# Output projection of an attention layer with its operands exchanged and y split in two float32r parts

## The chip, the cores and the metric

The program runs on one core of a Trainium2 chip. A core has four compute engines that run their own instruction streams and meet only at semaphores: TensorE (PE in the profile; its weight loads are the lane PEld), VectorE (DVE), ScalarE (ACT) and GpSimd (POOL). SyncE (SP) issues the DMAs. The metric is the device time of one execution in microseconds (us).

## The reference

Input x has 32 batches of 256 tokens of width 128. Five blocks follow each other, each on a layer norm of x and added to x: a tanh feed-forward, a linear attention, the tanh feed-forward again, a spectral (circulant) layer, a 16-head causal softmax attention, and the spectral layer again. The change touches the end of the softmax attention:

```
att = einsum('bhcq,bhCq->bhcC', q, k) / d_query        # 16 heads, 64 wide
p   = softmax(where(causal, att, -inf))
y   = einsum('bhcC,bhCv->bhcv', p, v)
z   = einsum('dvh,bhcv->bcd', W, y) * (sqrt(d_embed/d_value) / num_heads)
x   = x + z
```

So z of one batch is a product of a 256 x 1024 matrix y (tokens by heads and value channels) with a 1024 x 128 matrix W.

## The kernel before

The first four blocks run in some 260 us, in groups of 512 tokens. The softmax attention then takes the 32 batches one after another, in about 30 us each, and this is where most of the time lies. All operands stay in SBUF.

**Turns.** A batch has 8 pairs of heads, and each engine's program has 8 turns p = 0..7 for it (ACT and DVE are written in steps of two turns). In turn p of pair n = 8b + p, TensorE issues in this order: the q/k product of pair n + 2 (`qk_product`, 6 matmuls); one extra piece (values of this or the next batch in turns 0, 1, 6, 7; transposes of the next x in turn 2; the output projection of batch b - 1 in turns 3, 4, 5); the six transposes of the probabilities of pair n - 1 (`probs_transpose`); and in odd turns the scores of pairs n + 1 and n + 2 (`scores`), then the products of probabilities and values of pairs n - 2 and n - 1 (`products`). Every order is written out by hand; nothing is scheduled by a tool.

**The other engines.** DVE masks scores and finds their maxima (`mask_scores`, L527), takes the reciprocal of the sums (`inv_sum`, L535), copies two thirds of the transposed probabilities out of PSUM (`probs_T`, L542), makes the low part of q and k (`qk_low`, L513), and does the layer norms and additions to x. ACT does the exponentials (L809), the copies of q and k (L781, L787, L793, L794), one third of the transposed probabilities (L818) and the copy of y (`y_out`, L835). POOL multiplies the probabilities by the reciprocals (`scale_probs`, L333 and L335, 128x256 and 128x512) and does the small powers of the layer norms (L318, L345).

**Split operands.** TensorE's q/k and value products use float32r operands in two parts, `hi` (rounded) and `lo` (the rest), and three matmuls: hi by hi, hi by lo, lo by hi. The output projection before is in plain float32: `project_out` (L1120 to L1127) makes 16 matmuls for a batch. For each half of the tokens and each pair, 128 tokens of `yT` are the stationary operand and the 128 columns of `wz` move. The trace records each of these as two matmuls, so 32 records for a batch: 12 in turn 3, 12 in turn 4, 8 in turn 5. The result stands in PSUM with tokens on the partitions, as x does, and DVE adds it to x (`add_z`, L555).

**What orders the work around it.** `project_out` in turn 3 waits for `x_lo` of the next batch (DVE L507), as both use bank BANK_X; `x_lo` waits for ACT's `z_xT` copy (L849) and that for PE's transposes in turn 2. `y_out` of ACT writes a ring of two batches of y straight from PSUM. In turn 5 the spectral product of batch b - 2 (L1137, L1140) follows the projection, and DVE adds both results to x.

Of the kernel before, what the change touches and what calls it, by code (L numbers as in the profile page):

```python
# [17 lines left out]
G = 16  # L18
# [97 lines left out]
def build(nc, x, Wq, bq, Wd, bd, Wu, bu, Wo, bo, W1, W2, W3, ffn_bias, Q, K, V, W, w_re, w_im, fft_bias, dft, out):  # L116
    ctx = ExitStack()
    with ctx:
# [20 lines left out]
        space = sb("space", [P, 2 * BT * H * DV + 2 * PAIRS * T])  # L139
# [11 lines left out]
        wz = sb("wz", [P, PAIRS, D])  # L151
# [14 lines left out]
        xl_hi = sb("xl_hi", [P, 2, GW], F32R); xl_lo = sb("xl_lo", [P, 2, GW], F32R)  # L166
        eq = sb("eq", [P, GW]); rq = sb("rq", [P, GW]); ek = sb("ek", [P, GT, P])
        phq = sb("phq", [P, 2, GW]); phk = sb("phk", [P, GT, P])
# [3 lines left out]
        y0 = sb("y0", [P, GT, P]); yT0 = sb("yT0", [P, GW])  # L172
# [5 lines left out]
        pr = sb("pr", [P, 3, 2, 3, P])  # L178
        pT = sb("pT", [P, 2, 2, 3, P])

        vv = space[:, 0:2 * BT * H * DV].rearrange("p (r t n) -> p r t n", r=2, t=BT)
        y_ring = space[:, 2 * BT * H * DV:]
        yT = y_ring.rearrange("p (r a t) -> p r a t", r=2, a=PAIRS)
# [21 lines left out]
        pv_done = sem("pv_done"); y_ready = sem("y_ready")  # L205
# [49 lines left out]
        W_STEPS = ((0, 6), (6, 12), (12, 16))  # L255
# [28 lines left out]
        def _(pool):  # L284
# [5 lines left out]
            nc.gpsimd.memset(minus_1[:], -1.0)  # L290
            nc.gpsimd.memset(ones_bf[:], 1.0)
# [57 lines left out]

            def batch(b, jb, first=False, last=False):  # L350
# [7 lines left out]
            batches(pool, batch)  # L358
            z_inv_std(B - 1)
# [3 lines left out]
        def _(dve):  # L363
# [229 lines left out]

            def first_norm():
# [9 lines left out]
                          (1, 1): lambda: qk_weights_low(0), (1, G - LEAD - 1): lambda: qk_weights_low(1), (2, -LEAD): v_weights_low,  # L604
# [8 lines left out]
            def batch(b, jb, first=False, last=False):  # L613
                for p in range(0, PAIRS, 2):
# [22 lines left out]
                    if not (last and p == PAIRS - 2):  # L637
                        qk_low(n + 3, 1)
                    if p + 1 == W_TURN + 2 and not first:
# [3 lines left out]
                    probs_T(n, 0)  # L643
# [18 lines left out]
        def _(act):  # L662
# [601 lines left out]
```

## Time and profile before

| | us |
|---|---|
| median of 3 runs | 1256.41 (1256.25 to 1256.64) |
| the profiled execution | 1257.7 |
| its span, first to last instruction | 1254.8 |
| PE busy | 1187.8 (95%) |
| PEld busy | 1035.2 (83%) |
| DVE busy | 1023.7 (82%) |
| ACT busy | 1002.5 (80%) |
| POOL busy | 587.4 (47%) |

The granted clock of TensorE has a mean of 0.994, so it runs at the higher of its two levels nearly everywhere. DMA matters only in the first slice. How to read the rows below: a timeline row gives the start in us from the span's start, the duration in us, engine, line, operation, output and inputs, and in brackets how long the engine sat idle before it and what released it. A row of the chain gives start, length and what the chain was in. Matmul rows overlap, since they are pipelined; the chain's rows don't.

### The profile page before, as it was taken

The numbers are of one execution on the slowest core, as the hardware profiler recorded it, in microseconds if no ns is written. First come the engines' busy times: TensorE is split into PE (matmuls) and PEld (weight loads), VectorE is DVE, ScalarE is ACT, GpSimd is POOL, SyncE is SP. The second block draws the span as 40 slices with busy tenths as digits, with TensorE's granted clock in tenths as the row PEclk, the third lists the DMA queues.
The fourth block names the chain that finished last, engine by engine and source line by source line (L and its number), as shares of the span: only waits on it lengthen the run. The fifth ranks groups of instructions, "written<-read, shape, count | busy, mean of one in ns | idle before, by whom it ended". The sixth has DMA issues, their size and how long they took to land.

```text
span 1254.8 us, 38244 instructions
## 1 busy us (share of the span) xinstructions
PE 1187.8 (95%) x10824; PEld 1035.2 (83%) x10824; DVE 1023.7 (82%) x4874; ACT 1002.5 (80%) x3489; POOL 587.4 (47%) x912
## 2 busy tenths in 40 slices
PE   5699977789999999999999999999999999999996
PEld 4689966778888888888888888888888888888885
DVE  6888879977888888888888888888888888888874
ACT  4777648678888888888888888888888888888883
POOL 4822138634444444444444444444444444444442
PEclk9999999999999999999999999999999999999998
DMA  7000000000000000000000000000000000000000
GB/s 223 1 2 0 1 2 1 1 2 2 2 11 0 8 0 8 0 8 0 8 0 8 0 8 0 8 0 8 0 8 0 8 0 8 0 8 0 10 2 18
DMA packets 14540, 11.79 MB, mean 9 GB/s; under 512 B 725, under 2 KB 12569, under 8 KB 14489
## 3 DMA queue, kind: packets, MB, share of 16 engines
q1 hardware_dynamic: 14336, 11.19, 3.0%
q8 instruction: 22, 0.36, 0.1%
q14 instruction: 30, 0.24, 0.1%
q10 hardware_dynamic: 152, 0.00, 0.0%
HBM read 7.00 MB, written 4.19 MB: 9 GB/s over the span
## 4 chain that ended last, share of the span: by engine, by line
PE 82%; DVE 8%; issue 3%; POOL 2%; ACT 2%; DVEq 0%; DMA 0%; POOLq 0%; SPq 0%; ACTq 0%
PE ps L1115 15%; PE ps L1098 13%; PE ps L1124 10%; PE ps L1084 7%; PE ps L1067 7%; PE ps L1080 6%; PE ps L1068 5%; PE ps L1069 5%; PE ps L1106 2%; PE ps L1104 2%; PE ps L1105 2%; DVE bst L413 2%; POOL rstd L318 1%; DVE xn L426 1%; PE ps L1140 1%
## 5 line engine op out<-in xcount | busy, mean ns | idle before, releaser
L809 ACT ACTIVATE pr<-ps,neg_max 128x128 f32<-128x128 f32 (+1 forms) x1024 | 424.5, 429 | 111.4 <-DVE neg_max L527 111.4
L333 POOL TENSOR_TENSOR pr<-pr,rinv 128x256 f32<-128x256 f32 x256 | 157.4, 615 | 514.3 <-DVE rinv L535 514.3
L527 DVE CUSTOM_DVE_ANT_0 ps<-ps,mask 128x128 f32<-128x128 f32 (+1 forms) x1024 | 329.8, 392 | 0.4
L335 POOL TENSOR_TENSOR pr<-pr,rinv 128x512 f32<-128x512 f32 x256 | 266.2, 1040 | 0.0
L542 DVE COPY pT<-ps 128x512 f32<-128x512 f32 x256 | 176.2, 688 | 61.2 <-PE ps L1098 59.9
L809 ACT ACTIVATION_READ_ACCUMULATOR pr<-ps,neg_max 128x1 f32 x1024 | 217.8, 213 | 0.0
L1098 PE MATMUL ps<-ident,pr 128*128 128x128 f32 x1536 | 210.2, 273 | 2.2 <-POOL pr L335 0.9
L1115 PE MATMUL ps<-pT,space 128*64 128x256 f32 (+1 forms) x2048 | 196.2, 334 | 0.7 <-ACT pT L818 0.5
L1098 PEld LDWEIGHTS ps<-ident,pr 128*128 128x128 f32 x1536 | 179.4, 141 | 20.8 <-POOL pr L335 2.1
L1115 PEld LDWEIGHTS ps<-pT,space 128*64 128x64 f32 x2048 | 127.4, 137 | 56.0 <-issue 0.8
L1067 PE MATMUL ps<-x_hi,wqk_hi 128*128 128x256 f32 x512 | 167.8, 328 | 1.6 <-DVE x_lo L507 1.1
L527 DVE DVE_READ_ACCUMULATOR2_ANT neg_max<- 128x1 f32 x1024 | 145.4, 142 | 0.0
L1068 PE MATMUL ps<-x_lo,wqk_hi 128*128 128x256 f32 x512 | 144.1, 281 | 0.0
L1069 PE MATMUL ps<-x_hi,wqk_lo 128*128 128x256 f32 x512 | 144.0, 281 | 0.0
L1124 PE MATMUL ps<-wz,space 128*128 128x128 f32 x1024 | 132.1, 277 | 3.4 <-DVE x_lo L507 2.7
L1124 PEld LDWEIGHTS ps<-wz,space 128*128 128x128 f32 x1024 | 122.0, 191 | 8.6 <-issue 6.1
L1067 PEld LDWEIGHTS ps<-x_hi,wqk_hi 128*128 128x128 f32 x512 | 96.3, 188 | 24.6 <-issue 22.9
L818 ACT COPY pT<-ps 128x256 f32<-128x256 f32 x256 | 99.5, 389 | 17.3 <-PE ps L1098 14.8
L513 DVE TENSOR_TENSOR qk_lo<-ps,qk_hi 128x384 fp32r<-128x384 f32 x128 | 71.1, 556 | 41.9 <-ACT qk_hi L794 41.8
L1068 PEld LDWEIGHTS ps<-x_lo,wqk_hi 128*128 128x128 f32 x512 | 96.9, 189 | 0.0
L1069 PEld LDWEIGHTS ps<-x_hi,wqk_lo 128*128 128x128 f32 x512 | 96.1, 188 | 0.0
L1084 PE MATMUL ps<-qk_hi 64*128 64x256 f32 x512 | 94.1, 361 | 0.0
(173 smaller groups left out, 2622.7 us busy)
## 6 DMA issues: line engine op xcount, KB each, us to landing
out<-x_all SPq DMA_DIRECT2D x16, 256.0 KB, 2.3
x_all<-L_attn_x SPq DMA_DIRECT2D x1, 768.0 KB, 6.4
x_all<-L_attn_x SPq DMA_DIRECT2D x1, 512.0 KB, 4.2
space<-L_attn_Q SPq DMA_DIRECT2D x1, 512.0 KB, 13.3
space<-L_attn_K SPq DMA_DIRECT2D x1, 512.0 KB, 7.2
space<-L_attn_V SPq DMA_DIRECT2D x1, 512.0 KB, 7.9
space<-L_attn_W SPq DMA_DIRECT2D x1, 512.0 KB, 8.7
dft_s<-dft SPq DMA_DIRECT2D x1, 192.0 KB, 2.5
```

Of the source, the lines that this page charges most:

```text
L333: nc.gpsimd.tensor_tensor(pr[:, buf, :, 0, :], pr[:, buf, :, 0, :], r[:, :, 0:1].to_broadcast([P, 2, P]), ALU.mult)
L335: nc.gpsimd.tensor_tensor(pr[:, buf, :, 1:3, :].rearrange("p h b k -> p h (b k)"), pr[:, buf, :, 1:3, :].rearrange("p h b k -> p h (b k)") ...
L527: last = nc.vector.tensor_tensor_reduce(o, o, mask[:, T - w:T], -1.0, -MASKED, ALU.add, ALU.min, neg_max[:, j, 2 * h + qt:2 * h + qt + 1])
L542: nc.vector.tensor_copy(pT[:, j].rearrange("p h b q -> p (h b q)")[:, 0:512], ps[:, BANK_T, :]).then_inc(pTa_ready, 1)
L809: last = nc.scalar.activation(dst, ps[:, BANK_S + 2 * j + h, qt * P:qt * P + w], ACT.Exp, bias=neg_max[:, j, at:at + 1], scale=-1.0, accum ...
L1067: mm(o, wqk_hi[:, s, of_pair], x_hi[:, jb, :], start=True, stop=False, skip_group_check=True)
L1068: mm(o, wqk_hi[:, s, of_pair], x_lo[:, jb, :], start=False, stop=False, skip_group_check=True)
L1069: last = mm(o, wqk_lo[:, s, of_pair], x_hi[:, jb, :], start=False, stop=True, skip_group_check=True)
L1084: last = mm(ps[:, BANK_S + 2 * j + h, P:P + T], q[of_head, j, 0:P], key[of_head, j, P:], start=(k == 0), stop=(k == 2), skip_group_check=True)
L1098: last = tr(to, pr[:, buf, k // 3, k % 3, :], ident[:])
L1115: last = mm(ps[k * DV:(k + 1) * DV, BANK_Y, half * T + kt * P:(half + 1) * T], vv[:, jb, kt, h * DV:(h + 1) * DV], pT[:, j, k, 0:2, :] if ...
L1124: last = mm(ps[:, BANK_X, t * D:(t + 1) * D], yT[:, j, p, t * P:(t + 1) * P], wz[:, p, :], start=(p == 0), stop=(p == PAIRS - 1), skip_gro ...
```

## The change

- The projection is turned round: `wz_hi` or `wz_lo` of a pair (128x128) is stationary and all 256 tokens of y move. y comes in two float32r parts, `y_hi` and `y_lo`, so a pair takes three matmuls of 256 columns, a batch 24. The result o has its 128 output channels on the partitions, so ACT copies it to SBUF (`o_out`) and TensorE transposes it back in two transposes (`out_transpose`), now in turn 5 behind `probs_transpose`; the spectral product moves behind them.
- ACT's `y_out` copies PSUM to `y_raw`, a ring of two calls. POOL makes `y_hi` (multiply by one, output float32r) behind `scale_probs` of even turns and `y_lo` (subtract) behind that of odd turns: 4 calls each for a batch, of 128x512.
- On DVE `probs_T` of the even pair now comes ahead of `add_z` and `add_spectral` in turn 5. DVE makes `wz_lo` once, ahead of the third block (`w_low`).
- Several buffers of the first blocks now share space with those of the attention (`wz_lo` lies in `xl_lo`, `y_raw` in `phq`, `y_hi` over `xl_hi`).

```diff
+            def y_high(b, jb, p, calls, first=False):
+                pool.wait_ge(y_ready, count(calls))
+                if p == 1 and above_0(b - 1):
+                    pool.wait_ge(o_done, count(b - 1))
...
+                for to, at in places:
+                    last = nc.gpsimd.tensor_tensor(y_hi[:, to], y_raw[:, (p + 1) // 2 % 2, at],
+                                                   one[:].to_broadcast([P, at.stop - at.start]), ALU.mult)
+                last.then_inc(yhi_ready, 1)
+            def y_low(jb, p, calls):
+                pool.wait_ge(yhi_ready, count(calls))
+                for to, at in y_places(jb, p):
+                    last = nc.gpsimd.tensor_tensor(y_lo[:, to], y_raw[:, (p + 1) // 2 % 2, at], y_hi[:, to].bitcast(F32), ALU.subtract)
+                last.then_inc(ylo_ready, 1)
             def batch(b, jb, first=False, last=False):
                 for p in range(PAIRS):
                     scale_probs(b * PAIRS + p, p % 2, pr_of(p))
+                    if p == 0 and not first:
+                        y_high(b - 1, 1 - jb, PAIRS - 1, b * (PAIRS // 2))
+                    if p == 1 and not first:
+                        y_low(1 - jb, PAIRS - 1, b * (PAIRS // 2))
+                    if p > 0 and p % 2 == 0:
+                        y_high(b, jb, p - 1, b * (PAIRS // 2) + p // 2, first)
+                    if p > 1 and p % 2 == 1:
+                        y_low(jb, p - 2, b * (PAIRS // 2) + p // 2)
...
-                    nc.scalar.copy(y_ring[:, (at - 1) * T:(at + 1) * T], ps[:, BANK_Y, :]).then_inc(y_ready, 1)
...
+                if above_0(calls - 2):
+                    act.wait_ge(ylo_ready, count(calls - 2))
+                nc.scalar.copy(y_raw[:, (p + 1) // 2 % 2, :], ps[:, BANK_Y, :]).then_inc(y_ready, 1)
...
+            def o_out(b):
+                act.wait_ge(o_done, count(b + 1))
+                nc.scalar.copy(oT[:], ps[:, BANK_X, 0:T]).then_inc(o_ready, 1)
...
-            def project_out(b, j, steps, only=False):
-                pe.wait_ge(y_ready, count(PAIRS // 2 * (b + 1) + 1))
-                for k in range(*steps):
-                    t, p = k // PAIRS, k % PAIRS
-                    last = mm(ps[:, BANK_X, t * D:(t + 1) * D], yT[:, j, p, t * P:(t + 1) * P], wz[:, p, :],
-                              start=(p == 0), stop=(p == PAIRS - 1), skip_group_check=True)
+            def project_out(b, j, pairs):
+                calls = PAIRS // 2 * (b + 1)
+                for p in range(*pairs):
+                    if p in (0, 3, 5, 7):
+                        pe.wait_ge(ylo_ready, count(calls + (-2, -1, 0, 1)[(0, 3, 5, 7).index(p)]))
+                    of_pair = slice((j * PAIRS + p) * T, (j * PAIRS + p + 1) * T)
+                    mm(ps[:, BANK_X, 0:T], wz_hi[:, p, :], y_hi[:, of_pair], start=(p == 0), stop=False, skip_group_check=True)
+                    mm(ps[:, BANK_X, 0:T], wz_hi[:, p, :], y_lo[:, of_pair], start=False, stop=False, skip_group_check=True)
+                    last = mm(ps[:, BANK_X, 0:T], wz_lo[:, p, :], y_hi[:, of_pair], start=False, stop=(p == PAIRS - 1), skip_group_check=True)
```

TensorE in turn 5 of the last batch, before. A name such as `ps<-wz,space` gives the output and the operands; `x4` is four equal ones.

```order
L1069 MATMUL ps<-x_hi,wqk_lo 128x256
L1124 MATMUL ps<-wz,space 128x128 x4
L1137 MATMUL ps<-bias_bf,ones_bf 128x256
L1140 MATMUL ps<-circ,z_xT 128x128 x2
L1098 MATMUL ps<-ident,pr 128x128 x6
L1080 MATMUL ps<-qk_raw 128x128 x2
```

The same place now (`xl_lo` holds `wz_lo`; L1157 is `probs_transpose`, L1206 and L1209 the spectral product, L1139 the scores).

```order
L1128 MATMUL ps<-x_hi,wqk_lo 128x256
L1185 MATMUL ps<-y_hi,wz_hi 128x256
L1186 MATMUL ps<-y_lo,wz_hi 128x256
L1187 MATMUL ps<-y_hi,xl_lo 128x256
L1185 MATMUL ps<-y_hi,wz_hi 128x256
L1186 MATMUL ps<-y_lo,wz_hi 128x256
L1187 MATMUL ps<-y_hi,xl_lo 128x256
L1157 MATMUL ps<-ident,pr 128x128 x6
L1194 MATMUL ps<-ident,oT 128x128 x2
L1206 MATMUL ps<-bias_bf,ones_bf 128x256
L1209 MATMUL ps<-circ,z_xT 128x128 x2
L1139 MATMUL ps<-qk_raw 128x128 x2
```

The transposes of the probabilities moved ahead of the spectral product, and two more transposes stand between them. POOL around turn 6, before:

```order
L333 TENSOR_TENSOR pr<-pr,rinv 128x2x128
L335 TENSOR_TENSOR pr<-pr,rinv 128x2x256
L343 TENSOR_TENSOR z_veps<-z_mv,eps_t 128x2
L345 TENSOR_TENSOR z_rstd<-z_veps,half_neg 128x2
L333 TENSOR_TENSOR pr<-pr,rinv 128x2x128
L335 TENSOR_TENSOR pr<-pr,rinv 128x2x256
```

The same stretch now, from `y_low` of turn 5 to `y_low` of turn 7 (`phq` holds `y_raw`).

```order
L382 TENSOR_TENSOR y_lo<-phq,y_hi 128x512
L347 TENSOR_TENSOR pr<-pr,rinv 128x2x128
L349 TENSOR_TENSOR pr<-pr,rinv 128x2x256
L374 TENSOR_TENSOR y_hi<-phq,one 128x512
L357 TENSOR_TENSOR z_veps<-z_mv,eps_t 128x2
L359 TENSOR_TENSOR z_rstd<-z_veps,half_neg 128x2
L347 TENSOR_TENSOR pr<-pr,rinv 128x2x128
L349 TENSOR_TENSOR pr<-pr,rinv 128x2x256
L382 TENSOR_TENSOR y_lo<-phq,y_hi 128x512
```

One 128x512 operation with two SBUF inputs stands behind each `scale_probs`, and the small powers of turn 6 come after it.

## Rows read from the trace of the kernel before

**Rows 1.** Busy time by engine of the attention's steady stretch: us, busy us (instructions).

```profile
360.00:1200.00 840.00, 837.25 (x8039) 729.07 (x8039) 692.29 (x3384) 714.64 (x2643) 398.10 (x546) 1.00 0.02 4
```

**Rows 2.** The projection's line, 360 to 1240: what its engine waited for (us, times).

```profile
  DVE x_lo L507: 5.1, 28
  issue: 5.0, 13
```

**Rows 3.** Waits between engines, 360 to 1240: us in total, times, longest.

```profile
ACT pr L809 <- DVE neg_max L527: 98.7, 114, 1.3
DVE x_lo L507 <- ACT z_xT L849: 41.1, 28, 1.5
DVE qk_lo L513 <- ACT qk_hi L794: 36.0, 86, 1.0
DVE space L551 <- PE ps L1106: 14.9, 42, 0.7
```

**Rows 4.** The chain that ended last, one batch: start us, us, what.

```profile
703.92 1.34 PE ps L1124 x12
...
705.91 0.12 PE ps L1067
...
706.63 0.89 PE ps L1124 x8
...
715.23 0.66 PE ps L1098 x6
...
726.73 0.22 PE ps L1132 x2
```

**Rows 5.** Timeline of DVE in the same batch, turns 6 to 3.

```profile
713.19 0.69 DVE L551 COPY space<-ps 128x512 f32<-128x512 f32 x1 [0.18 <-PE ps L1106]
...
714.45 0.55 DVE L513 TENSOR_TENSOR qk_lo<-qk_raw,qk_hi 128x384 fp32r<-128x384 f32 x1
714.92 0.60 DVE L426 TENSOR_SCALAR xn<-x_all,mv,rstd 128x128 f32 x2
...
721.59 0.55 DVE L513 TENSOR_TENSOR qk_lo<-qk_raw,qk_hi 128x384 fp32r<-128x384 f32 x1
...
728.00 0.43 DVE L507 TENSOR_TENSOR x_lo<-ps,x_hi 128x256 fp32r<-128x256 f32 x1 [1.47 <-ACT z_xT L849]
```

**Rows 6.** Timeline of ACT in the same batch.

```profile
706.74 0.37 ACT L793 COPY qk_odd<-ps 128x256 f32<-128x256 f32 x1 [0.42 <-PE ps L1069]
...
717.47 0.37 ACT L809 ACTIVATE pr<-ps,neg_max 128x128 f32<-128x128 f32 x1 [0.52 <-DVE neg_max L527]
...
722.04 0.49 ACT L794 CAST qk_hi<-ps 128x384 fp32r<-128x384 f32 x1
...
724.61 0.37 ACT L809 ACTIVATE pr<-ps,neg_max 128x128 f32<-128x128 f32 x1 [0.52 <-DVE neg_max L527]
```

**Rows 7.** Timeline of POOL in the same batch.

```profile
709.74 0.61 POOL L333 TENSOR_TENSOR pr<-pr,rinv 128x256 f32<-128x256 f32 x1 [3.42 <-DVE rinv L535]
...
712.36 0.61 POOL L333 TENSOR_TENSOR pr<-pr,rinv 128x256 f32<-128x256 f32 x1 [1.01 <-DVE rinv L535]
712.93 1.04 POOL L335 TENSOR_TENSOR pr<-pr,rinv 128x512 f32<-128x512 f32 x1
...
714.21 0.70 POOL L345 TENSOR_TENSOR z_rstd<-z_veps,half_neg 128x2 f32<-128x2 f32 x1
```

**Rows 8.** Durations by line, 360 to 1240: ns min/median/max, first and last start.

```profile
L513 DVE TENSOR_TENSOR qk_lo<-qk_raw,qk_hi x114: 548/548/550, 361.1 to 1227.2; 128x384 fp32r<-128x384 f32 x114
...
L579 DVE TENSOR_SCALAR z_xn<-x_all,z_mv,z_rstd x58: 316/341/634, 382.4 to 1236.6; 128x128 f32 x52, 128x128 f32<-128x128 f32 x6
```

**Rows 9.** Timelines of POOL and DVE at turn 0 of an earlier batch.

```profile
627.49 0.61 POOL L333 TENSOR_TENSOR pr<-pr,rinv 128x256 f32<-128x256 f32 x1 [1.19 <-DVE rinv L535]
...
627.57 0.61 DVE L579 TENSOR_SCALAR z_xn<-x_all,z_mv,z_rstd 128x128 f32 x1 [0.17 <-issue]
```

**Rows 10.** DVE groups by form, 60 to 320: xcount | busy us, mean ns | idle.

```profile
L592 DVE TENSOR_TENSOR v_lo<-space,v_hi 128x1024 fp32r<-128x1024 f32 x1 | 1.2, 1215 | 0.0
```

**Rows 11.** Timeline of all engines at the end.

```profile
1242.44 3.81 PE L1124 MATMUL ps<-wz,space 128*128 128x128 f32 x32 [0.56 <-ACT space L843]
```

More of the change, by code:

```diff
@@ L150, in build @@
         v_hi = sb("v_hi", [P, H * DV], F32R); v_lo = sb("v_lo", [P, H * DV], F32R)
-        wz = sb("wz", [P, PAIRS, D])
+        wz_hi = sb("wz_hi", [P, PAIRS, D], F32R);
+        y_hi = sb("y_hi", [P, 2 * PAIRS * T], F32R); y_lo = sb("y_lo", [P, 2 * PAIRS * T], F32R)
+        oT = sb("oT", [P, T]); one = sb("one", [P, 1])
         half_neg = sb("half_neg", [P, GT]); eps_t = sb("eps_t", [P, GT])
@@ L358, in _ @@
             batches(pool, batch)
+            y_high(B - 1, 1, PAIRS - 1, B * (PAIRS // 2))
+            y_low(1, PAIRS - 1, B * (PAIRS // 2))
+            pool.wait_ge(y_ready, B * (PAIRS // 2) + 1)
+            nc.gpsimd.tensor_tensor(y_hi[:, (2 * PAIRS - 1) * T:], y_raw[:, 1, 0:T], one[:].to_broadcast([P, T]), ALU.mult).then_inc(yhi_ready, 1)
+            pool.wait_ge(yhi_ready, B * (PAIRS // 2) + 1)
+            nc.gpsimd.tensor_tensor(y_lo[:, (2 * PAIRS - 1) * T:], y_raw[:, 1, 0:T], y_hi[:, (2 * PAIRS - 1) * T:].bitcast(F32),
+                                    ALU.subtract).then_inc(ylo_ready, 1)
             z_inv_std(B - 1)
@@ L879, in batch @@
                         qk_high_odd(n + 3)
+                    if p + 1 == W_TURN + 2 and not first:
+                        o_out(b - 1)
                     exp_head(n + 1, 1, 1, pr_of(p + 1))
@@ L890, in _ @@
             batches(act, batch)
[L891 removed]
+            y_out(B - 1, PAIRS - 1, B * (PAIRS // 2))
             z_xT_out(B - 2)
@@ L894, in _ @@
             last_y_out()
+            o_out(B - 1)
             z_xT_out(B - 1, B + 1)
@@ L1118, in products, with out_transpose @@
                 last.then_inc(pv_done, 1)
-            def project_out(b, j, steps, only=False):
-                pe.wait_ge(y_ready, count(PAIRS // 2 * (b + 1) + 1))
-                for k in range(*steps):
-                    t, p = k // PAIRS, k % PAIRS
-                    last = mm(ps[:, BANK_X, t * D:(t + 1) * D], yT[:, j, p, t * P:(t + 1) * P], wz[:, p, :],
-                              start=(p == 0), stop=(p == PAIRS - 1), skip_group_check=True)
-                if (only or not above_0(b)) and steps[1] == BT * PAIRS:
+            def project_out(b, j, pairs):
[7 more added lines that the diff above has]
+                    last = mm(ps[:, BANK_X, 0:T], wz_lo[:, p, :], y_hi[:, of_pair], start=False, stop=(p == PAIRS - 1), skip_group_check=True)
+                if pairs[1] == PAIRS:
+                    last.then_inc(o_done, 1)
+            def out_transpose(b, only=False):
+                pe.wait_ge(o_ready, count(b + 1))
+                for t in range(BT):
+                    last = tr(ps[:, BANK_X, t * D:(t + 1) * D], oT[:, t * P:(t + 1) * P], ident[:])
+                if only or not above_0(b):
                     last.then_inc(w_done, 1)
@@ L1199, in batch @@
                         probs_transpose(n - 1, 1 - j, pr_of(p - 1), b * (PAIRS // 2) + p // 2)
+                    if p == W_TURN + len(W_PAIRS) - 1 and not first:
+                        out_transpose(b - 1)
+                        if above_0(b - 1):
+                            spectral_product(b - 2)
                     if p % 2 == 1:
@@ L1218, in _ @@
             pe.wait_ge(out_ready, B - 1)
-            project_out(B - 1, 1, (0, BT * PAIRS), only=True)
+            project_out(B - 1, 1, (0, PAIRS))
+            out_transpose(B - 1, only=True)
             spectral_transpose(B - 1)
```

75 lines of the change are left out of this document (41 added, 34 removed).

## The prediction

> **What bounds the kernel now.** I read the busy times first, then the chain of waits, then the waits, then the timelines of one batch. In the steady stretch of the attention TensorE is busy for 837 of 840 us, with the granted clock at 1.00, that is 2.4 GHz [rows 1]. So a matmul record that goes away there is worth its share of the chain. The busy share alone misleads, though: the other engines sit close behind. From 713 us on, one batch shows it. DVE waits 0.18 us for TensorE ahead of `values_copy` in turn 6 and then runs without a gap to the masks of the next pair, for which ACT waits 0.52 us [rows 5, 6]. ACT then runs without a gap to `qk_hi` at 722.04 (ends 722.53), DVE's low part and masks follow, ACT waits for them again until 724.61 [rows 6], and its run ends in `z_xT`, for which DVE's `x_lo` waits until 728.00 [rows 5]. The projection in turn 3 waits for just that `x_lo`: each of 28 batches has a wait on it, with 5.1 us on L507 and 5.0 us of issue in all over the two lanes of TensorE [rows 2]. So from turn 6 to turn 3 there is a second chain (DVE, ACT, DVE, ACT, DVE) of 15.3 us that is as long as TensorE's own work there. In turns 3 to 5 both wait for TensorE (ACT's 0.42 us ahead of `qk_odd` is one such place [rows 6]).
>
> **TensorE's work.** Removed for each batch: 12 + 12 + 8 records of L1124. By the chain, 12 take 1.34 us and 8 take 0.89 us, so 1.34 + 1.34 + 0.89 = 3.57 us [rows 4]. Added: 24 float32r matmuls of 256 columns. The nearest rows are the q/k products, of the same form: six of them stand between 705.91 and 706.63, so 0.12 us each and 2.88 us for 24. The two transposes of o cost what two transposes of z cost, 0.22 us [rows 4]. The sum is 3.57 - 3.10 = 0.47 us less: 0.26 us in each of turns 3 and 4 (nine matmuls for twelve records), and in turn 5 0.72 + 0.22 against 0.89, 0.05 us more. Bounds: the nine could cost as much as the twelve records if moving two different streams against one weight block were slower (no row of q/k shows that), and 0.49 us is the other end. I take 0.46 us, for 31 batches: 14.3 us. The 32nd projection is in the tail.
>
> **ACT.** It gets `o_out`, a copy of 128x256 from PSUM, 0.37 us as L793 [rows 6]. It stands behind `qk_hi` of the odd pair. With TensorE half a microsecond earlier, ACT no longer waits 0.42 us there, reads o when the last projection matmul is done (0.72 us behind the q/k product), and is ready when TensorE has made its six transposes (0.66 us, [rows 4]). I cost the wait of `out_transpose` at nothing: its cover is those 0.66 us, against 0.37 us plus two semaphores. If the cover were gone, it would be up to 0.4 us a batch, and behind the waiting transposes stand the spectral product and the scores. The delayed exponentials end ahead of the wait for the next maxima, which is the longest of a batch, up to 1.3 us [rows 3]. `y_out` keeps its size. Its new wait for `ylo_ready` looks two calls back, one whole batch half earlier, so nothing.
>
> **DVE in turn 5.** `add_z` now waits longer, since the spectral product stands behind the transposes, but the copy of the probabilities is done first. The masks of turn 6 start some 0.34 us earlier than before and the values copy 0.46 us, since its wait of 0.18 us [rows 5] shrinks. So the second chain starts 0.46 us earlier too.
>
> **POOL.** It gets 8 operations of 128x512 a batch. L335 has this form with a broadcast input and takes 1.04 us [rows 7]: 8.3 us a batch. A doubled price (float32r output is not shown on POOL) is the other bound; down, a cheaper one gains nothing. POOL's scaling takes 0.57 + 1.04 = 1.61 us. The pair scaled at 709.74 is followed by the next at 712.36, 2.62 us later [rows 7]; with `y_low` between them, 1.61 + 1.0 = 2.6 us fit exactly. Behind even pairs there is 3.4 us. The probabilities of the even pair are ready at 713.97, and TensorE takes them at 715.23 [rows 4], so 1.2 us of slack take up what `y_low` may be longer. So POOL's time itself costs nothing.
>
> **What POOL does to DVE.** This is the term that decides. In turn 6 `y_high` starts behind the scaling, at about 713.9 on the old clock, and lasts to about 715. DVE's `qk_lo` of 714.45, which has two SBUF inputs, and the `xn` behind it lie in that time [rows 5]. Today POOL is in short operations then. Both lie on the second chain, with no gap in front of them. The trace has one kind of collision: at 627.49 POOL starts L333, at 627.57 DVE starts `z_xn`, and it takes 0.61 us instead of the median 0.34 us [rows 8, 9], so 0.29 us at most (634 against 341 ns). Against that, `qk_lo` lies inside POOL's `z_rstd` (714.21 to 714.91 [rows 7]) and takes 548 to 550 ns in all 114 cases [rows 8]: two elements of POOL do not disturb it. For 512 elements no row exists. Lower bound 0; upper bound the part of 1.04 us that is left when `qk_lo` comes, some 0.65 us. I take 0.29 us, the only collision with a number. In turn 0 `qk_lo` at 721.59 meets the next `y_high`, but DVE waits for ACT's `qk_hi` right after it (36.0 us in 86 waits, 0.42 us each [rows 3]; 0.16 us is left there in turn 0), and in turn 2 that wait is longer. I cost these two at nothing; if the cover is short, up to 0.3 us. In turn 4 POOL is done before `qk_lo`.
>
> The Trainium skill, "SBUF — State Buffer", section "Who interferes with whom", speaks against this change: a VectorE instruction with two SBUF inputs contends with a GpSimd instruction that reads SBUF, and whoever comes first has the shared port pair for the whole instruction. By that rule the collision in turn 6 is the upper bound of the above and the case is the slower rival below. The row of `z_rstd` against `qk_lo` does not agree with a hold over the whole instruction, that of `z_xn` agrees with some hold.
>
> **Once only.** `w_low` has the form of `v_lo`, 1.2 us on DVE [rows 10], between blocks in which DVE is nearly full: bounds 0 and 1.2, I take 1.0. In the tail 32 records of 3.81 us [rows 11] become 24 of 2.9 us, of which 21 run while ACT (0.37 us) and POOL (twice 0.61 us) finish the last y; `o_out` and two transposes add 0.8 us: -0.3 us, between -0.9 and +1.
>
> **The sum.** 31 x (-0.46 + 0.29) = -5.3, +1.0, -0.3: -4.6 us. The profiled execution (1257.7, span 1254.8) would become 1253.1, span 1250.2. It is 1.3 us above the median of 1256.4, so the median becomes **1251.8 us**. Own range of this case: collisions of 0.2 to 0.42 us, 1248 to 1256.
>
> **Rivals.**
> - *The whole saving arrives (no collision counts).* For: 114 `qk_lo` undisturbed beside `z_rstd`, and the second chain starts as early as TensorE. Against: `z_xn`. Then 31 x -0.46 + 0.7 = -13.6 us: 1242.8.
> - *DVE is held behind `y_high` (slower).* In turn 6 `qk_lo` waits 0.65 us, in turn 0 it or the `z_xn` behind it some 0.1 to 0.3 us beyond the cover. The second chain is then 0.3 to 0.5 us longer than now in spite of the earlier start, and TensorE waits for `x_lo` in turn 3 and for the transposed probabilities in turns 1 and 7. It decides from collisions of 0.46 us in sum. 31 x 0.3 + 0.7 = +10: 1266.4; with 0.5, 1272.6.
> - *The gain is given back without a collision.* The second chain is already as long as TensorE's, so `o_out` or the late `add_z` keep DVE from starting earlier: -0.46 becomes about 0, with `w_low` on top: 1256 to 1258. For: ACT is busy for 715 of 840 us [rows 1], and every batch waits on `x_lo` already. Against: both engines wait for TensorE in turns 4 and 5, by more than what is added.
>
> **How the numbers follow.** Forecast 0.32, whole saving 0.32, held 0.22, given back 0.14. A measurement of this kernel can tell about 0.2%, 2.5 us. Faster by more: 0.32 plus three quarters of the forecast, 0.56. Slower by more: the held case and a little of the third, 0.25. The same: 0.19. For eight in ten the range takes all of the first two and most of the held case's lower part: 1240 to 1268.
>
> **What would show it.** In the profile after: the projection's three lines at 0.12 us a record in the chain, 2.9 us a batch; `y_hi` and `y_lo` at 1.04 us on POOL, POOL at 70 to 75%; `qk_lo` from SBUF with a median above 548 ns and two groups of durations, the long one in turns 6 and 0 (unchanged durations speak for the whole saving, 1.0 us and more for the held case); TensorE's idle time ahead of the projection for `x_lo` above 10 us (it stays in the whole-saving case). The step fails if TensorE's busy time does not fall by 13 to 15 us, or if `out_transpose` shows a wait for `o_ready`, or if the scaled probabilities come late.

## The result, and the profile after

The changed kernel takes 1261.7 us (median of 6 runs, 1259.5 to 1262.2), against 1256.3 us (1255.8 to 1257.0) of the kernel before in the same session: a ratio of 1.0036, 95% interval 1.0025 to 1.0048. It is slower by 0.2 to 0.5%. The forecast was 1251.8 us, faster; the time lies in its range (1240 to 1268), but on the other side of the kernel before, between the forecast and the rival "DVE is held behind `y_high`". The profiled execution took 1260.7 us with a span of 1259.0, 4.2 us more than the span of before.

TensorE did what it was changed for. This is the chain that ended last, at the start of a projection (start us, us, what):

```profile
731.42 0.43 DVE x_lo L557
731.85 0.04 issue
731.90 0.38 PE ps L1185
732.28 0.12 PE ps L1186
732.40 0.12 PE ps L1187
732.52 0.11 PE ps L1185
```

After the first one, each float32r matmul of the projection stands 0.12 us behind the one ahead of it, as forecast. The busy time of the steady stretch (as [rows 1]: PE, PEld, DVE, ACT, POOL):

```profile
360.00:1200.00 840.00, 832.72 (x7828) 714.63 (x7828) 729.32 (x3378) 706.07 (x2647) 663.68 (x792) 1.00 0.02 4
```

TensorE's clock is granted in full, as before, and TensorE is busy for 4.5 us less than in [rows 1]. It now waits. Over the whole span its busy time fell by 4.0 us (1187.8 to 1183.8), not by the 13 to 15 that the prediction named as its sign; experiments 1, 3, 4 and 7 below, in which next to nothing is held, show the full fall (1171.1 to 1172.8). A record of such a matmul is 0.28 us long and the next one starts 0.12 us behind it, so a pause of up to 0.16 us leaves no idle time, and the busy time hides part of the loss. DVE is busy for 37 us more though its list of instructions in a batch is the same. The row that answers to [rows 8], with min/median/max in ns, shows where most of that comes from:

```profile
L563 DVE TENSOR_TENSOR qk_lo<-qk_raw,qk_hi x114: 546/966/1284, 362.6 to 1232.2; 128x384 fp32r<-128x384 f32 x114
```

It was 548/548/550. The timelines of POOL and of DVE in turn 6 show how one `qk_lo` gets so long (start us, us; the pair that answers to [rows 5, 7]). In this text a hold is the time by which one engine's instruction is lengthened beside another's.

```profile
716.95 1.04 POOL L374 TENSOR_TENSOR y_hi<-phq,one 128x512 fp32r<-128x512 f32 x1
717.95 0.51 POOL L357 TENSOR_TENSOR z_veps<-z_mv,eps_t 128x2 f32<-128x2 f32 x1
```

```profile
717.20 1.20 DVE L563 TENSOR_TENSOR qk_lo<-qk_raw,qk_hi 128x384 fp32r<-128x384 f32 x1
718.33 0.59 DVE L476 TENSOR_SCALAR xn<-x_all,mv,rstd 128x128 f32 x2
718.84 0.55 DVE L563 TENSOR_TENSOR qk_lo<-ps,qk_hi 128x384 fp32r<-128x384 f32 x1
```

POOL is done at 717.99. DVE's `qk_lo`, which started 0.25 us behind it, ends 0.41 us later, at 718.40, and takes 1.20 us in place of 0.55. The `xn` behind it (0.59 us) and the `qk_lo` that reads PSUM (0.55 us) take what they took before. The chain of waits goes through just these rows:

```profile
717.20 0.99 DVE qk_lo L563
718.20 0.13 issue
718.33 0.35 DVE xn L476 x2
718.68 0.17 issue
718.84 0.56 DVE qk_lo L563
719.40 0.12 issue
719.52 0.49 PE ps L1139 x4
```

The chain as a whole has changed with it. By engine it was TensorE for 82% and DVE for 8% before; now:

```profile
PE 53%; DVE 15%; ACT 14%; issue 13%; DMA 1%; POOL 1%; DVEq 1%; ACTq 1%; SPq 1%; POOLq 0%
```

In turn 6, what comes late first is TensorE's scores of turn 7, directly behind DVE's second `qk_lo`. PEld's timeline has the same wait, 0.33 us; in turns 3 and 5 this group (`qk_odd`) has none, in turn 1 it has 0.08:

```profile
719.51 0.31 PEld L1139 LDWEIGHTS ps<-qk_odd 64*128 64x128 f32 x4 [0.33 <-issue]
```

By turn (27 batches each) the mean `qk_lo` is 0.76 us in turn 2, 0.73 in turn 4, 1.19 in turn 6 and 1.24 in turn 0. To see which of these cost time I took marks: from the start of `x_lo` to the first q/k matmul of each turn behind it, mean over 18 batches, in us. The last column is the time of a batch.

```
             turn 4  turn 5  turn 6  turn 7  turn 0  turn 1  turn 2   batch
before         5.56    8.28   14.09   16.17   21.22   23.30   28.35   30.65
after          5.29    7.74   13.63   15.71   21.14   23.22   28.47   30.82
```

TensorE gains 0.27 us in turn 3, 0.27 in turn 4, and gives 0.08 back in turn 5: 0.46 us up to turn 6. Between the starts of turns 7 and 0 it loses 0.38 of them, and between those of turns 1 and 2 another 0.20.

### The profile page after: what moved, and what is told of

The parts are those of the page before. It is cut to its first block, busy times and chain, and to the rows that moved or that the text cites. A ratio compares the mean times of both kernels' runs of the same rounds, so it can differ in the third digit from the quotient of the medians.

```text
span 1259.0 us, 38464 instructions
## 1 busy us (share of the span) xinstructions
PE 1183.8 (94%) x10632; PEld 1020.5 (81%) x10632; DVE 1071.5 (85%) x4875; ACT 997.0 (79%) x3506; POOL 897.5 (71%) x1203
## 4 chain that ended last, share of the span: by engine, by line
PE 53%; DVE 15%; ACT 14%; issue 13%; DMA 1%; POOL 1%; DVEq 1%; ACTq 1%; SPq 1%; POOLq 0%
PE ps L1174 9%; ACT pr L866 8%; PE ps L1157 8%; PE ps L1143 4%; PE ps L1139 4%; PE ps L1126 3%; DVE qk_lo L563 3%; PE ps L1185 3%; PE ps L1186 2%; PE ps L1187 2%; PE ps L1127 2%; PE ps L1128 2%; PE ps L1004 2%; DVE xn L476 1%; DVE pT L592 1%
## 5 line engine op out<-in xcount | busy, mean ns | idle before, releaser
L866 ACT ACTIVATION_READ_ACCUMULATOR pr<-ps,neg_max 128x1 f32 x1024 | 220.8, 216 | 0.0
L1157 PE MATMUL ps<-ident,pr 128*128 128x128 f32 x1536 | 209.8, 273 | 2.5 <-POOL pr L349 1.1
L1157 PEld LDWEIGHTS ps<-ident,pr 128*128 128x128 f32 x1536 | 178.8, 141 | 20.4 <-POOL pr L349 2.5
L382 POOL TENSOR_TENSOR y_lo<-phq,y_hi 128x512 fp32r<-128x512 f32 (+1 forms) x144 | 167.2, 1166 | 0.1
L374 POOL TENSOR_TENSOR y_hi<-phq,one 128x512 fp32r<-128x512 f32 (+1 forms) x143 | 140.8, 989 | 0.0
L577 DVE DVE_READ_ACCUMULATOR2_ANT neg_max<- 128x1 f32 x1024 | 140.6, 137 | 0.0
L563 DVE TENSOR_TENSOR qk_lo<-qk_raw,qk_hi 128x384 fp32r<-128x384 f32 x128 | 124.9, 975 | 2.5 <-ACT qk_hi L844 2.5
L875 ACT COPY pT<-ps 128x256 f32<-128x256 f32 x256 | 103.7, 405 | 0.9 <-PE ps L1157 0.8
L329 POOL TENSOR_TENSOR neg_mean<-mv,minus 128x4 f32<-128x4 f32 x64 | 17.9, 280 | 121.0 <-DVE mv L468 105.1
```

Of the source, the lines that this page charges most:

```text
L382: last = nc.gpsimd.tensor_tensor(y_lo[:, to], y_raw[:, (p + 1) // 2 % 2, at], y_hi[:, to].bitcast(F32), ALU.subtract)
L563: nc.vector.tensor_tensor(qk_lo[:, j], qk_raw[:, P:] if j == 0 else ps[:, BANK_QK, P:], qk_hi[:, j].bitcast(F32), ALU.subtract).then_inc(q ...
L577: last = nc.vector.tensor_tensor_reduce(o, o, mask[:, T - w:T], -1.0, -MASKED, ALU.add, ALU.min, neg_max[:, j, 2 * h + qt:2 * h + qt + 1])
L866: last = nc.scalar.activation(dst, ps[:, BANK_S + 2 * j + h, qt * P:qt * P + w], ACT.Exp, bias=neg_max[:, j, at:at + 1], scale=-1.0, accum ...
L1157: last = tr(to, pr[:, buf, k // 3, k % 3, :], ident[:])
```

## The experiments

Eight kernels were run, the first four in one session (the kernel before: 1257.1 us), the last four in another (1257.2 us). Ratios are to the kernel before of the same session. "A" is the theory that POOL's `y_high` holds `qk_lo`; the others are named in each expectation.

**1. `y_high` on two columns.** Take away the suspected cause and keep the rest. `y_hi` is set to zero once at the start, so this kernel leaves out the projection's true result.

```
-                for to, at in places:
-                    last = nc.gpsimd.tensor_tensor(y_hi[:, to], y_raw[:, (p + 1) // 2 % 2, at],
-                                                   one[:].to_broadcast([P, at.stop - at.start]), ALU.mult)
+                for to, at in places[-1:]:
+                    last = nc.gpsimd.tensor_tensor(y_hi[:, to.start:to.start + 2], y_raw[:, (p + 1) // 2 % 2, at.start:at.start + 2],
+                                                   one[:].to_broadcast([P, 2]), ALU.mult)
```

> The changed kernel, but POOL's y_high handles 2 columns instead of 512 (y_hi is otherwise left at zero, so the projection's result is left out); y_low stays whole. Theory A (VectorE's qk_lo with two SBUF inputs is blocked while y_high runs, and that lengthens the chain DVE-ACT-DVE-ACT-DVE from turn 6 to turn 3): qk_lo from SBUF is back at 548 ns in nearly all 114 cases, a batch gets 0.5 to 0.65 us shorter than in the changed kernel, time 1242 to 1247 us. Theory B (the gain is given back in turn 5 by ACT's o_out and the late add_z): 1259 to 1262 us, qk_lo short all the same. Theory C (POOL is late with the scaled probabilities): something between, with less waiting of TensorE for POOL's L349; y_low is still 1.29 us, so 1250 to 1259.

Measured: 1241.9 us (1240.7 to 1242.0), ratio 0.9875 (0.9858 to 0.9891). `qk_lo` is back at 546/548/553 ns, and a batch takes 0.487 us less than before. A holds, and the TensorE term of the prediction (0.46 us) is right. ACT's `o_out`, its new order and `y_low` cost nothing once `y_high` is out of the way.

**2. The kernel before with one more POOL operation.** Add the suspected cause and nothing else.

```
                     scale_probs(b * PAIRS + p, p % 2, pr_of(p))
+                    if p % 2 == 0:
+                        if above_0(b * (PAIRS // 2) + p // 2):
+                            pool.wait_ge(extra_done, count(b * (PAIRS // 2) + p // 2))
+                        nc.gpsimd.tensor_tensor(extra[:], extra_in[:], half_neg[:, 0:1].to_broadcast([P, 512]), ALU.mult).then_inc(extra_done, 1)
```

> The kernel before, with one POOL operation more behind the scaling of each even turn: 128x512 float32 with a broadcast second input, SBUF to SBUF, on data that nobody else uses. Projection, ACT and DVE are as before. Theory A: qk_lo from SBUF goes from 548 ns to 0.9 to 1.3 us, 0.65 us more in turn 6 (whole on the chain) and 0.2 us beyond the cover in turn 0, less 0 to 0.2 us of slack: 0.6 to 0.85 us a batch, 1275 to 1283 us. Theory B: 1256 to 1258 us, as nothing of turn 5 is touched. Theory C: 1.04 us more on POOL behind even pairs, where it idles 3 us: 1256 to 1257 us.

Measured: 1264.5 us (1262.9 to 1266.4), ratio 1.0058 (1.0041 to 1.0076), +0.28 us a batch. The direction is A's, the size is not: A wanted 1275 to 1283. `qk_lo` takes 0.95 us in turn 6 and 1.11 in turn 0, less than in the changed kernel, and some of that hold costs nothing. Experiment 8 and the account below it take this up.

**3. `y_high` as a write only.** Does it need POOL's time, or its reads? This kernel too leaves out the true result.

```
+                nc.gpsimd.tensor_tensor(tiny[:], half_neg[:, 0:2], half_neg[:, 2:4], ALU.mult)
                 for to, at in places:
-                    last = nc.gpsimd.tensor_tensor(y_hi[:, to], y_raw[:, (p + 1) // 2 % 2, at],
-                                                   one[:].to_broadcast([P, at.stop - at.start]), ALU.mult)
+                    last = nc.gpsimd.memset(y_hi[:, to].bitcast(F32), 0.0)
```

> The changed kernel, but y_high is a POOL operation on 2 columns that carries the wait, and then a memset of the 512 columns of y_hi, which writes SBUF and reads nothing (y_hi is zero, so the projection's result is left out). If only POOL's reads hold up a DVE operation with two SBUF inputs (the Trainium skill, 'SBUF - State Buffer', 'Who interferes with whom'): qk_lo stays at 548 ns, at most xn and z_xn are longer, 1243 to 1249 us. If any use of SBUF by POOL holds it up: qk_lo is longer in turns 6 and 0 by what is left of the memset, 1250 to 1262 us.

Measured: 1241.2 us (1240.8 to 1243.3), ratio 0.9871 (0.9854 to 0.9887); `qk_lo` 546/548/550 ns. The two do overlap, and DVE is not delayed. Timelines of POOL and DVE in turn 6:

```profile
709.54 0.52 POOL L376 MEMSET y_hi<- 128x512 f32 x1
```

```profile
709.66 0.55 DVE L564 TENSOR_TENSOR qk_lo<-qk_raw,qk_hi 128x384 fp32r<-128x384 f32 x1
```

The overlap here is 0.40 us. By the account below an operation with reads would delay `qk_lo` by 0.26 us over it, and the row is within 5 ns of what it was. In 28 of the 114 cases the overlap is above 0.3 us (up to 0.49), and these take 546 to 550 ns. So the first reading of the expectation holds (the time is below its range), and this is the stronger for the overlap being long: a write alone is not enough to hold DVE.

**4. `y_high` later.** The whole result, with the same POOL operations, but behind DVE's low parts.

```
                     scale_probs(b * PAIRS + p, p % 2, pr_of(p))
-                    if p == 0 and not first:
-                        y_high(b - 1, 1 - jb, PAIRS - 1, b * (PAIRS // 2))
...
-                    if p > 0 and p % 2 == 0:
-                        y_high(b, jb, p - 1, b * (PAIRS // 2) + p // 2, first)
...
                     if p == Z_TURN and not first:
                         z_inv_std(b - 1)
+                    if p % 2 == 0 and not (last and p == PAIRS - 2):
+                        pool.wait_ge(qklo_ready, count(b * PAIRS + (p + 4)))
+                    if p == 0 and not first:
+                        y_high(b - 1, 1 - jb, PAIRS - 1, b * (PAIRS // 2))
+                    if p > 0 and p % 2 == 0:
+                        y_high(b, jb, p - 1, b * (PAIRS // 2) + p // 2, first)
```

> The changed kernel, whole result, but POOL's y_high of each even turn waits until DVE has made qk_lo of the next two pairs, so it runs beside mask and copy work from PSUM and ahead of the next (odd) scaling. Theory A: qk_lo from SBUF back at 548 ns in turns 6, 0 and 2; the saving of TensorE arrives, less what the late odd scaling costs (slack 1.9 us against up to 0.3 us; y_low then pushes the even scaling by up to 0.5 us of 1.2 us slack, and z_xn of turn 0 may be held for 0.6 us, which VectorE spends waiting for TensorE anyway): 1243 to 1250 us. Theory B: 1259 to 1262 us. Theory C: 1262 us or more, with waits of TensorE for L349.

Measured: 1241.1 us (1240.4 to 1242.7), ratio 0.9874 (0.9857 to 0.9890), 1.3% faster than before and better than A's range. In turn 6:

```profile
708.39 1.09 POOL L359 TENSOR_TENSOR z_rstd<-z_veps,half_neg 128x2 f32<-128x2 f32 x1
710.07 1.04 POOL L374 TENSOR_TENSOR y_hi<-phq,one 128x512 fp32r<-128x512 f32 x1 [0.58 <-DVE qk_lo L565]
```

```profile
708.38 0.55 DVE L565 TENSOR_TENSOR qk_lo<-qk_raw,qk_hi 128x384 fp32r<-128x384 f32 x1
708.84 0.60 DVE L478 TENSOR_SCALAR xn<-x_all,mv,rstd 128x128 f32 x2
709.36 0.55 DVE L565 TENSOR_TENSOR qk_lo<-ps,qk_hi 128x384 fp32r<-128x384 f32 x1
```

`y_high` waits for the low part of the odd pair, `qk_lo` takes 0.55 us again, and it is POOL that is held now and then: `z_rstd`, which starts 0.01 us behind `qk_lo`, takes 1.09 us in place of 0.70. POOL has the time: at this place its work costs nothing.

**5 and 6. Later in turn 6 alone, and in turn 0 alone.** Each is the changed kernel with the edit of experiment 4 in one of the four turns. Experiment 5, behind `z_inv_std`:

```
-                    if p > 0 and p % 2 == 0:
+                    if p in (2, 4):
                         y_high(b, jb, p - 1, b * (PAIRS // 2) + p // 2, first)
...
+                    if p == 6:
+                        if not last:
+                            pool.wait_ge(qklo_ready, count(b * PAIRS + (p + 4)))
+                        y_high(b, jb, p - 1, b * (PAIRS // 2) + p // 2, first)
```

Experiment 6, at the same place, where the call of turn 0 is taken from its old one:

```
+                    if p == 0 and not first:
+                        pool.wait_ge(qklo_ready, count(b * PAIRS + (p + 4)))
+                        y_high(b - 1, 1 - jb, PAIRS - 1, b * (PAIRS // 2))
```

> The whole result, as the changed kernel, but in turn 6 alone y_high stands behind POOL's last short operations and waits for DVE's low part of the odd pair; in turns 0, 2 and 4 it stays where it was. The y_high delayed in all turns gave 1241.1, the changed kernel 1261.7. Theory A (the 0.65 us of turn 6 and the 0.18 us beyond the cover in turn 0 are separate losses, each on the chain): qk_lo at 0.55 us in turn 6 and 1.2 in turn 0, -0.485 + 0.18 = -0.3 us a batch against the kernel before, 1246 to 1249. Theory D (turn 0 has its cover only because turn 6 was late; without turn 6 the chain arrives earlier there and the whole 0.7 us of turn 0 counts): +0.2 us a batch, about 1260. Theory E (turn 6 holds the whole loss, turn 0 is covered): 1241 to 1243.

> The whole result, as the changed kernel, but in turn 0 alone y_high waits for DVE's low part of the odd pair; in turns 2, 4 and 6 it stays. Theory A (separate losses): turn 6 keeps its 0.65 us, turn 0 gives back 0.18 us: -0.485 + 0.65 = +0.165 us a batch would be all of what the changed kernel shows, so at most 0.18 us a batch is gained, 1256 to 1260. Theory D (whichever comes first takes the slack): as the changed kernel, 1260 to 1262. Theory F (turn 0 is what costs): 1245 or less.

Measured: 1252.4 us (1251.4 to 1254.4), ratio 0.9965 (0.9951 to 0.9979), with turn 6 clean; 1252.8 us (1251.7 to 1253.9), ratio 0.9968 (0.9955 to 0.9980), with turn 0 clean. None of the theories is met. Each turn alone costs some 11 us over the 1241.1 of experiment 4, and both together 20.6: the losses nearly add, but in two almost equal halves, not as 0.65 and 0.18 us a batch.

**7. `y_high` in four pieces.** At its old place, but four operations of 128x128.

```
-                for to, at in places:
+                for to, at in [(slice(o.start + k, o.start + k + P), slice(i.start + k, i.start + k + P))
+                               for o, i in places for k in range(0, i.stop - i.start, P)]:
```

> The whole result, as the changed kernel, but every y_high is four operations of 128x128 in place of one of 128x512, at the same place; about 0.33 us each, 1.3 us in all in place of 1.04. y_low is unchanged. Theory A (a POOL operation with SBUF inputs holds DVE's two-input operation until its own end, and lets it in between two operations): qk_lo in turns 6 and 0 waits for one piece at most, 0.55 + 0.1 to 0.4 us, and the time falls to 1244 to 1253. Theory G (POOL keeps DVE out as long as it has work queued with SBUF inputs, or both share the port by turns): qk_lo stays at 1.2 us or gets longer, as the pieces together do, 1262 to 1270.

Measured: 1241.7 us (1241.0 to 1242.6), ratio 0.9878 (0.9861 to 0.9894). That is A's direction, below its 1244 to 1253, and G falls. All of the gain comes back with no wait and nothing moved. POOL and DVE in turn 6:

```profile
708.81 1.79 POOL L375 TENSOR_TENSOR y_hi<-phq,one 128x128 fp32r<-128x128 f32 x4
```

```profile
709.07 0.56 DVE L564 TENSOR_TENSOR qk_lo<-qk_raw,qk_hi 128x384 fp32r<-128x384 f32 x1
709.55 0.77 DVE L477 TENSOR_SCALAR xn<-x_all,mv,rstd 128x128 f32 x2
710.25 0.54 DVE L564 TENSOR_TENSOR qk_lo<-ps,qk_hi 128x384 fp32r<-128x384 f32 x1
```

and the durations of these four pieces, min/median/max in ns:

```profile
L375 POOL TENSOR_TENSOR y_hi<-phq,one x4: 396/401/720, 708.8 to 710.2; 128x128 fp32r<-128x128 f32 x4
```

`qk_lo` comes 0.26 us behind the start of `y_high`, just as in the changed kernel, and takes 0.56 us. One of the pieces takes 720 ns where the others take 400: now POOL waits for DVE. So the hold belongs to one instruction and ends with it. A little of it is left (by turn `qk_lo` has a mean of 0.57 to 0.66 us), and it costs nothing. It is no matter of POOL's load, which is highest here: 738 of 840 us.

**8. The kernel before with both kinds of operation.** Experiment 2, and in odd turns a second one:

```
+                    if p % 2 == 1:
+                        if above_0(b * (PAIRS // 2) + p // 2):
+                            pool.wait_ge(extra_2_done, count(b * (PAIRS // 2) + p // 2))
+                        nc.gpsimd.tensor_tensor(extra_2[:], extra_in[:], extra_in[:], ALU.subtract).then_inc(extra_2_done, 1)
```

> The kernel before with both kinds of operation on POOL and nothing else of the change: in every even turn a 128x512 tensor_tensor with a broadcast input behind the scaling, and in every odd turn one with two full SBUF inputs and a float32r output. The results go nowhere. With the first kind alone it took 1264.5, +0.28 us a batch, and its hold in turn 6 was 0.40 us, since the odd turn's operation was missing and the even scaling ended earlier. Theory A (the odd operation pushes the even one later against qk_lo, so the whole collision of the changed kernel comes back): qk_lo at 1.2 us in turns 6 and 0, and the time of the changed kernel plus the 0.487 us a batch that TensorE saves there: 1256.4 + 31 x 0.65 = 1276.6; 1272 to 1280. Theory H (what the changed kernel loses depends on its own order on ACT and DVE, not on POOL's operations): as with the first kind alone, 1263 to 1267.

Measured: 1264.5 us (1262.5 to 1265.6), ratio 1.0056 (1.0038 to 1.0074), +0.28 us a batch, with the same `qk_lo` by turn as experiment 2. A's extension (1272 to 1280) falls: the odd operation pushes nothing. H named the right time (1263 to 1267), but not for the reason it gave: of what differs between the two kernels, most of the longer hold is in POOL's operations after all. The timelines of turn 6:

```profile
718.82 1.04 POOL L358 TENSOR_TENSOR extra<-extra_in,half_neg 128x512 f32<-128x512 f32 x1
```

```profile
719.33 0.95 DVE L523 TENSOR_TENSOR qk_lo<-qk_raw,qk_hi 128x384 fp32r<-128x384 f32 x1
```

Here `qk_lo` starts 0.51 us behind POOL's operation, in the changed kernel 0.25 us. In these two batches, from `x_lo` on, the changed kernel has `qk_lo` at 16.52 us against 16.98, and `y_high` at 16.26 against 16.46: `qk_lo` comes 0.46 us earlier, POOL's operation only 0.20. POOL's own rows show why. The odd turn's operation and the scaling behind it, in the changed kernel and then here:

```profile
714.13 1.29 POOL L382 TENSOR_TENSOR y_lo<-phq,y_hi 128x512 fp32r<-128x512 f32 x1
715.38 0.61 POOL L347 TENSOR_TENSOR pr<-pr,rinv 128x256 f32<-128x256 f32 x1
```

```profile
716.20 1.04 POOL L362 TENSOR_TENSOR extra<-extra_in 128x512 fp32r<-128x512 f32 x1
717.25 0.61 POOL L335 TENSOR_TENSOR pr<-pr,rinv 128x256 f32<-128x256 f32 x1
```

The scaling needs DVE's reciprocals. It starts 0.08 us after them here and in the kernel before, but 0.27 us after them in turn 6 of the changed kernel (means of 27 batches): `y_low` takes 1.29 us, and the scaling and `y_high` behind it stand 0.19 us late. The operation of this experiment takes 1.04 us and is done just in time, so it pushes nothing. So most of the longer hold (0.64 us against 0.40) comes from the length of `y_low`, and the small rest from DVE's reciprocals, which come only some 0.4 us earlier. An estimate from these rows: with a `y_low` of 1.04 us the hold in turn 6 would be 0.45 us and its loss about 0.2 us in place of 0.38. No run tried this.

**The account.** The same marks for the experiments (us):

```
                           turn 6  turn 7  turn 0  turn 1  turn 2   batch
4, both turns clean         13.63   15.72   20.76   22.85   27.89   30.17
7, four pieces              13.62   15.71   20.75   22.84   27.89   30.16
5, turn 6 clean             13.62   15.70   20.74   22.83   28.21   30.57
6, turn 0 clean             13.63   15.71   21.13   23.21   28.25   30.53
8, before and both          14.09   16.17   21.34   23.42   28.54   30.93
```

With the extra length of `qk_lo` over 0.55 us as the hold, a turn's loss is its hold less a fixed cover:

```
                  hold   loss  how read                                   cover
turn 6, after     0.64   0.38  turn 0: 21.14 - 20.76                       0.26
turn 6, exp. 6    0.64   0.37  21.13 - 20.76                               0.27
turn 6, exp. 8    0.40   0.12  21.34 - 21.22 (before)                      0.28
turn 0, after     0.69   0.27  batch: 30.82 - 30.17, less 0.38             0.42
turn 0, exp. 5    0.81   0.40  30.57 - 30.17                               0.41
turn 0, exp. 8    0.56   0.16  30.93 - 30.65, less 0.12                    0.40
```

Three values from three kernels agree within 0.02 us in each turn. The cover in turn 0 lies at DVE's wait for ACT's `qk_hi`, ahead of the second `qk_lo`. The 0.42 us of [rows 3] is not its size, though: that is the mean over turns 2, 4 and 0, which have 0.58, 0.42 and 0.22 us. By the medians of experiments 4 and 5, the first `qk_lo` of turn 0 takes 0.85 us longer, but the second one starts only 0.43 and the masks 0.39 us later: the second `qk_lo` now starts 0.08 us ahead of the end of `z_xn`, where there was a pause of 0.28 us. What is left of the waits of all turns in the changed kernel and in experiment 4 (360 to 1200: us, times, longest):

```profile
DVE qk_lo L563 <- ACT qk_hi L851: 17.1, 55, 0.6
```

```profile
DVE qk_lo L565 <- ACT qk_hi L853: 34.4, 84, 0.6
```

In turn 0 of the changed kernel nothing is left of it. In turn 2 the cover is larger: in experiment 6 a mean hold of 0.53 us stands there, and the marks show no loss behind it.

The cover in turn 6 has no such wait on DVE. It lies between DVE's second `qk_lo` and the scores: in experiment 4 that `qk_lo` ends at 709.91 and the second scores start at 710.40, in the changed kernel 719.39 and 719.52, so 0.36 us of slack are used up. What the cover falls short of that, 0.1 us, fits the delayed scores themselves: that group of four takes 0.49 us against 0.38, in the changed kernel and in experiment 4:

```profile
719.52 0.49 PE L1139 MATMUL ps<-qk_odd 64*128 64x128 f32 x4
```

```profile
710.40 0.38 PE L1141 MATMUL ps<-qk_odd 64*128 64x128 f32 x4
```

The covers also explain experiments 2 and 8: a hold of 0.40 and 0.56 us, less 0.28 and 0.40.

## Why the prediction was wrong, point by point

The step that failed is "What POOL does to DVE": a hold of 0.29 us in turn 6, whole on the chain, and none that counts in turn 0. Measured were holds of 0.64 and 0.69 us, with losses of 0.38 us a batch in turn 6 and 0.27 in turn 0. Over 31 batches that is 2.8 and 8.4 us more than the sum had, so turn 0 is the larger part of the miss.

- **TensorE's work, 0.46 us a batch: right.** 0.46 us up to turn 6 with the changed kernel, 0.487 us a batch where nothing is given back (experiments 1, 4, 7). The second stream against one weight block costs nothing extra.
- **ACT and `out_transpose` at nothing: right.** `oT` takes 0.39 us; no wait of `out_transpose` (L1194) for it is among the waits before the tail, and the late `add_z` cost nothing either. The rival "given back without a collision" falls with experiments 1 and 4.
- **POOL's time at nothing: right for TensorE only.** `y_low` takes 1.29 us and not the 1.04 of the row that was used. The slack of 1.2 us ahead of TensorE takes that up, as forecast, but `y_high` comes 0.19 us later against `qk_lo` in turn 6, and that lengthens the hold. The prediction had checked POOL's lateness against TensorE alone.
- **What POOL does to DVE: this step failed, by its size.** The prediction had the right place, the right two instructions and two bounds (0 and 0.65 us) and took 0.29 us, the length of the only collision in the trace. The hold is 0.64 us. That it meets the upper bound is partly luck: the bound was what is left of `y_high` when `qk_lo` comes, which is 0.56 us on the old clock and 0.79 us in the changed kernel (717.20 to 717.99), and the hold is 0.14 us less than that. `z_xn` [rows 9] was no measure of a hold: it says how long one DVE instruction met one POOL instruction, and that hangs on where they meet. What could be carried over was the rule, not the number: 627.49 + 0.61 = 628.10 is POOL's end there, and `z_xn` ends at 628.18, right behind it.
- **Turn 0 "at nothing": wrong by the same number.** With a hold of 0.29 us the cover of 0.41 us is enough; with 0.69 us it isn't, and 0.27 us a batch are lost. This is as large as the whole term that the sum had. That the mean of 0.42 us which the prediction gave is near the cover is chance: the wait in turn 0 is shorter.
- **"With no gap in front of them": wrong the other way.** The second chain, DVE and ACT by turns (713.19 to 728.43, so 15.2 us and not 15.3), isn't what binds in turn 6. The scores of turn 7 wait for `qk_lo` first, and there 0.27 us are free. Had the sum taken 0.65 us in turn 6 whole, it would have been too dark: experiment 2's expectation, made with that reading, missed by 10 us. So the 0.29 us of the sum was near the net loss of turn 6 (0.38) because two errors offset each other, a hold too short and a cover not seen.
- **Turn 4 "is done before `qk_lo`": wrong.** `y_hi` runs from 708.56 to 709.59, `qk_lo` starts at 709.23 and takes 0.78 us. It costs nothing: the marks up to turn 6 are those of the clean kernels.
- **The sum.** 31 x (-0.487 + 0.38 + 0.27) = +5.1 us; `x_lo` of the last batch less that of the first moves by 5.88 - 0.64 = +5.2. The first `x_lo` is 0.64 us late; the excess is there at 168 us already, ahead of `w_low`. `w_low` takes 1.2 us as `v_lo` does (taken at 1.0); ACT is 1.25 us late behind it, at 187 us, and 0.63 again from 223 us on, so it is made up for there. Where the first 0.64 us come from was not followed up. The tail behind the last `x_lo` is 1.7 us shorter, of which 0.46 is that batch's own projection and 0.45 the end from the last product to `z_xn`'s transposes; the rest was not followed up. Together +4.2 us of span.
- **The rivals.** "Held behind `y_high`" had the mechanism, with 0.3 to 0.5 us a batch net where 0.17 were measured, since it knew no cover in turn 6. Its signs came true: `qk_lo` at 1.0 us and more, and TensorE's waits on the projection's line up from 10.1 us [rows 2] to 12.5. "The whole saving arrives" (1242.8 us) is what experiments 1, 4 and 7 are: 1241.1 to 1241.9.

The rule of the Trainium skill ("SBUF — State Buffer", section "Who interferes with whom"), that a VectorE instruction with two SBUF inputs and a GpSimd instruction that reads SBUF keep each other out for the whole instruction, agrees with the traces in both directions, but for 0.14 us by which the two may overlap at no cost: `qk_lo` behind a 128x512 operation of POOL ends 0.41 us after it in turns 6 and 0, and POOL's piece of 400 ns takes 720 behind `qk_lo`. It should have been given more weight than the row of `z_rstd`, which stays an exception that no run explains: `qk_lo` starts beside it, not quite inside it as the prediction has it (714.45 to 715.00 against 714.21 to 714.91), and is not held, in all 28 batches.

The changed kernel with `y_high` in four pieces (1241.7 us) or placed later (1241.1 us) is 1.2 to 1.3% faster than the kernel before and 1.6% faster than the changed one.

## What to carry to other kernels

A saving on the busiest engine arrives only if no one else is moved into the way: work shifted to an engine that is half idle is free in that engine's time, and can still lengthen a neighbour's instruction that is on the chain. Price such a collision by where the two will meet (the other's end, less this one's start), and compare it with the cover in each turn separately, taken from that turn's own waits and not from a mean. Ask of every new operation what it pushes: here a quarter of a microsecond more on one instruction was covered on one side and moved the next one into a neighbour on the other. Where it bites, cut the offending instruction into short pieces or let it wait for the neighbour; both gave back all of it here.

## What the runs showed of the hardware

- A POOL tensor_tensor of 128x512 from SBUF makes a DVE tensor_tensor with two SBUF inputs end 0.41 us after POOL's end (1.19 to 1.20 us against 0.55 in turn 6). The hold is thus the overlap less 0.14 us: an overlap of 0.14 us, as with the first piece of experiment 7, costs nothing. This holds within 0.01 us for all 456 `qk_lo` of the changed kernel and experiments 2, 5, 6 and 8 that start inside a POOL tensor_tensor of 256 or 512 columns, over overlaps of 0.10 to 0.99 us.
- A POOL tensor_tensor of two columns (`z_rstd`, 0.70 us) is an exception in this direction: `qk_lo` starts 0.24 us into it in the kernel before and takes 548 to 550 ns.
- It works both ways: POOL's `z_veps` takes 0.51 us in place of 0.20, `z_rstd` 1.09 in place of 0.70, a piece of `y_high` 0.72 in place of 0.40, all beside `qk_lo`.
- A DVE operation with one of two inputs in PSUM is not held: the second `qk_lo` of turn 6 in experiment 7 starts at 710.25 beside the last piece, which ends at 710.60, and takes 0.54 us. `xn`, with one SBUF tensor and two columns of scalars, gets longer: 0.77 us for the two beside the pieces, in place of 0.60.
- POOL's memset of 128x512 takes 0.52 us and did not delay `qk_lo` in experiment 3, over overlaps of up to 0.49 us (28 cases above 0.3 us, 546 to 550 ns).
- POOL's subtract of two different 128x512 tensors with a float32r output takes 1.29 us, one of a tensor with itself 1.04 us. `y_hi`, also with a float32r output, takes 1.04 us, so the output's type is not what makes the 0.25 us; the rest was not tried apart.
